# Adapter weights fetched in four chunks beside four tiles, in a routed LoRA kernel

## What is computed

```python
def reference(x, itok, weight):            # x (128, 32, 512), itok (128,), weight (8, 512, 512)
    w = weight[itok]                       # ids are drawn from 3 to 7
    return x + jnp.einsum('bsi,boi->bso', x, w)
```

## Time and profile before

| | |
|---|---|
| median of 3 runs | 105.68 us (105.65 to 105.77) |
| profiled execution | 105.87 us |
| its span, first to last instruction | 104.3 us |
| TensorE busy (matmuls) | 98.8 us, 95% |
| ScalarE busy | 55.9 us, 54% |
| VectorE busy | 52.9 us, 51% |
| GpSimd busy | 42.3 us, 41% |
| moved by DMA | 22.92 MB, mean 220 GB/s |
| mean granted TensorE clock | 0.993 of full |

### The profile page before, as it was taken

How to read it: one execution, slowest core, us unless ns; L and a number is a source line. 1 busy time by engine, 2 the same in 40 slices (tenths; PEclk the granted TensorE clock), 3 DMA queues, 4 the chain that set the end, 5 groups by cost and what they waited for, 6 DMA issues and landing times.

```text
span 104.3 us, 2280 instructions
## 1 busy us (share of the span) xinstructions
PE 98.8 (95%) x437; PEld 79.5 (76%) x437; DVE 52.9 (51%) x107; ACT 55.9 (54%) x103; POOL 42.3 (41%) x58
## 2 busy tenths in 40 slices
PE   5989999999999999999999999999999999999950
PEld 2548888888888888888887888888888888888830
DVE  1569773694076803782248831784477217850000
ACT  5076244594249806592439942695497426952220
POOL 6646305208330761247312774058425530586000
PEclk9999999999999999999999999999999999999997
DMA  1984799939996999789993587648736585354533
GB/s 15 316 229 122 208 233 338 322 86 341 357 316 203 231 356 360 221 140 333 390 314 109 174 259 262 203 126 253 241 106 204 182 262 155 103 188 149 182 101 101
DMA packets 24944, 22.92 MB, mean 220 GB/s; under 512 B 3121, under 2 KB 20018, under 8 KB 24930
## 3 DMA queue, kind: packets, MB, share of 16 engines
q1 hardware_dynamic: 19298, 9.45, 33.2%
q0 software_dynamic: 2608, 8.06, 20.2%
q10 hardware_dynamic: 3024, 5.24, 16.5%
HBM read 17.30 MB, written 8.91 MB: 251 GB/s over the span
## 4 chain that ended last, share of the span: by engine, by line
PE 86%; DMA 3%; ACTq 2%; ACT 2%; SPq 1%; POOL 1%; issue 1%; DVE 1%; POOLq 0%
PE out_ps L527 86%; DMA x_raw<-in_x 3%; ACTq L189 2%; ACT out_tile L344 1%; SPq L179 1%; SPq L185 0%; ACT xt_hi L315 0%; DVE first_from_end L400 0%; POOL ones L253 0%; POOL earlier L257 0%; POOL from_end L250 0%; DVE ids_bf L402 0%; DVE first_at L405 0%; POOL eights L259 0%; POOL key_base L250 0%
## 5 line engine op out<-in xcount | busy, mean ns | idle before, releaser
L287 POOL DMA_INDIRECT out<-out_tile,row_of x31 | 34.9, 1127 | 49.5 <-ACT out_tile L344 45.3
L527 PE MATMUL out_ps<-w_hi,xt_hi 128*128 (+1 forms) x136 | 53.1, 390 | 0.4 <-ACT xt_hi L315 0.4
L527 PE MATMUL out_ps<-w_lo,xt_hi 128*128 (+1 forms) x136 | 52.9, 389 | 0.0
L442 DVE TENSOR_TENSOR xt_lo<-x_raw,xt_hi 128x512 fp32r<-128x512 f32 x34 | 23.7, 696 | 32.2 <-ACT xt_hi L315 31.6
L527 PE MATMUL out_ps<-w_hi,xt_lo 128*128 (+1 forms) x136 | 36.6, 389 | 0.0
L315 ACT ACTIVATE xt_hi<-x_raw 128x512 fp32r<-128x512 f32 (+1 forms) x35 | 21.5, 616 | 26.1 <-DMA x_raw<-in_x 25.9
L527 PEld LDWEIGHTS out_ps<-w_hi,xt_hi 128*128 128x128 f32 x136 | 25.5, 188 | 6.3 <-issue 1.1
L527 PEld LDWEIGHTS out_ps<-w_hi,xt_lo 128*128 128x128 f32 x136 | 25.5, 188 | 5.3
L527 PEld LDWEIGHTS out_ps<-w_lo,xt_hi 128*128 128x128 f32 x136 | 25.5, 188 | 5.3
L337 ACT ACTIVATE w_hi<-w_raw 128x512 fp32r<-128x512 f32 x32 | 18.2, 621 | 12.2 <-DVE w_raw L176 9.1
L344 ACT ACTIVATE out_tile<-out_ps 128x512 f32<-128x512 f32 x34 | 19.9, 585 | 6.1 <-PE out_ps L527 6.1
(11 more groups left out here) (60 smaller groups left out, 10.3 us busy)
## 6 DMA issues: line engine op xcount, KB each, us to landing
x_raw<-in_x SPq DMA_DIRECT2D x130, 64.0 KB, 2.7
w_raw<-in_weight ACTq DMA_DIRECT2D x6, 1024.0 KB
w_raw<-in_weight ACTq DMA_DIRECT2D x6, 256.0 KB, 4.0
w_raw<-in_weight SPq DMA_DIRECT2D x2, 256.0 KB, 3.1
out<-out_tile,row_of POOLq DMA_INDIRECT x31, 3.9
out<-out_tile ACTq DMA_DIRECT2D x6, 64.0 KB, 1.9
out<-out_tile SPq DMA_DIRECT2D x6, 64.0 KB, 2.0
x_raw<-in_x POOLq DMA_DIRECT2D x4, 64.0 KB, 2.7
```

The source lines that it names most:

```text
L287: nc.gpsimd.indirect_dma_start(out=out_rows, out_offset=bass.IndirectOffsetOnAxis(ap=row_of[:, t:t + 1], axis=0), in_=out_tile[n][:, :], i ...
L442: nc.vector.tensor_tensor(xt_lo[t % XT_BUFS][:, :, :, :], x_raw[t % X_BUFS][:, :, :, :].rearrange("p m c r -> p c m r"), xt_hi[t % XT_BUFS ...
L527: return nc.tensor.matmul(out_ps[n][:, :], lefts[left][k][:, c, :, :].rearrange("p m r -> p (m r)"), rights[right][:, bass.ds(rank, 1), c, ...
```

## The change

Ranks 2 to 7 are loaded chunk by chunk, in four steps from `NEEDED_FROM[j] - 6` to `NEEDED_FROM[j] - 3`, each with a wait for the same chunk of the adapter two ranks earlier. The diagonal of these ranks is added two chunks at a time, ahead of chunk 0 and ahead of chunk 2. SyncE issues chunk 3 of rank 0 right behind chunk 1. The semaphores of weight loads are now one for each buffer and chunk.

```diff
-        w0_loaded = [sem(f"w0_loaded{c}") for c in range(CHUNKS)]
-        w1_loaded = [sem(f"w1_loaded{c}") for c in range(CHUNKS)]
-        w_loaded = [sem(f"w_loaded{n}") for n in range(W_BUFS)]
+        w_loaded = [[sem(f"w_loaded{n}_{c}") for c in range(CHUNKS)] for n in range(W_BUFS)]
...
         def wait_w_loaded(eng, rank, c):
-            if rank == 0:
-                eng.wait_ge(w0_loaded[c], 16)
-            elif rank == 1:
-                eng.wait_ge(w1_loaded[c], 16)
-            else:
-                eng.wait_ge(w_loaded[rank % W_BUFS], 16 * (rank // W_BUFS))
+            eng.wait_ge(w_loaded[rank % W_BUFS][c], 16 * (rank // W_BUFS + 1))
...
-            return [j for j in range(2, ADAPTERS) if t == NEEDED_FROM[j] - 5]
+            return [(j, c) for j in range(2, ADAPTERS) for c in range(CHUNKS) if t == NEEDED_FROM[j] - 6 + c]
...
         @block.sync
         def _(sp):
             sp.dma_start(ids_row[:, :], ids.rearrange("(o b) -> o b", o=1)).then_inc(ids_row_loaded, 16)
-            load_rank_0(sp, (1,))
+            load_rank_0(sp, (1, 3))
...
             load_tile(0, first[0:2])
-            load_rank_0(sp, (3,))
             load_tile(1, first[SEQS:2 * SEQS])
...
-            def load_rank(j):
+            def load_chunk(j, c, key):
                 n = j % W_BUFS
-                k = act.value_load(sorted_key[0:1, j:j + 1], min_val=0, max_val=MAX_KEY)
-                act.wait_ge(w_lo_ready, (j - W_BUFS) * CHUNKS + CHUNKS)
-                act.dma_start(w_raw[n][:, :, :], w_t[bass.ds(k & (KEY - 1), 1), :, :, :].rearrange("a c p o -> p (a c) o"),
-                              cond=k >= KEY, max_dma_last_dim=4 * D).then_inc(w_loaded[n], 16)
+                act.wait_ge(w_lo_ready, (j - W_BUFS) * CHUNKS + c + 1)
+                act.dma_start(w_raw[n][:, c, :], w_t[bass.ds(key & (KEY - 1), 1), c, :, :].rearrange("a p o -> (a p) o"),
+                              cond=key >= KEY).then_inc(w_loaded[n][c], 16)
...
-                    act.wait_ge(w_plus_one, c + 1 if j == 1 else CHUNKS + j - 1)
+                    act.wait_ge(w_plus_one, c + 1 if j == 1 else CHUNKS + 2 * (j - 2) + c // 2 + 1)
...
-                for j in weight_loads(t):
-                    load_rank(j)
+                for j, c in weight_loads(t):
+                    if c == 0:
+                        key = act.value_load(sorted_key[0:1, j:j + 1], min_val=0, max_val=MAX_KEY)
+                    load_chunk(j, c, key)
...
-                    elif c == 0:
+                    elif j > 1 and c % 2 == 0:
                         wait_w_loaded(dve, j, c)
-                        add_one(nc.vector, j, slice(0, CHUNKS)).then_inc(w_plus_one, 1)
+                        wait_w_loaded(dve, j, c + 1)
+                        add_one(nc.vector, j, slice(c, c + 2)).then_inc(w_plus_one, 1)
                     split_weight(j, c)
```

More of the change, by code:

```diff
@@ L151, in load_rank_0 @@
             for c in chunks:
-                eng.dma_start(w_raw[0][:, c, :], w_t[FIRST_ADAPTER, c, :, :]).then_inc(w0_loaded[c], 16)
+                eng.dma_start(w_raw[0][:, c, :], w_t[FIRST_ADAPTER, c, :, :]).then_inc(w_loaded[0][c], 16)
         def wait_w_loaded(eng, rank, c):
-            if rank == 0:
-                eng.wait_ge(w0_loaded[c], 16)
-            elif rank == 1:
-                eng.wait_ge(w1_loaded[c], 16)
-            else:
-                eng.wait_ge(w_loaded[rank % W_BUFS], 16 * (rank // W_BUFS))
+            eng.wait_ge(w_loaded[rank % W_BUFS][c], 16 * (rank // W_BUFS + 1))
         def weight_steps(t):
@@ L304, in load_rank_1 @@
                 act.dma_start(w_raw[1][:, c, :], w_t[bass.ds(a, 1), c, :, :].rearrange("a p o -> (a p) o")
-                              ).then_inc(w1_loaded[c], 16)
-            def load_rank(j):
+                              ).then_inc(w_loaded[1][c], 16)
+            def load_chunk(j, c, key):
                 n = j % W_BUFS
-                k = act.value_load(sorted_key[0:1, j:j + 1], min_val=0, max_val=MAX_KEY)
-                act.wait_ge(w_lo_ready, (j - W_BUFS) * CHUNKS + CHUNKS)
-                act.dma_start(w_raw[n][:, :, :], w_t[bass.ds(k & (KEY - 1), 1), :, :, :].rearrange("a c p o -> p (a c) o"),
-                              cond=k >= KEY, max_dma_last_dim=4 * D).then_inc(w_loaded[n], 16)
+                act.wait_ge(w_lo_ready, (j - W_BUFS) * CHUNKS + c + 1)
+                act.dma_start(w_raw[n][:, c, :], w_t[bass.ds(key & (KEY - 1), 1), c, :, :].rearrange("a p o -> (a p) o"),
+                              cond=key >= KEY).then_inc(w_loaded[n][c], 16)
             def x_hi_part(t, chunks):
```

## The result

The change makes the kernel slower by half a per cent: 106.37 us median against 106.03 us, 22 runs of each. The ratio of the executions compared is 1.005 with a 95% interval of 1.0028 to 1.0072, that is 0.30 to 0.76 us. The forecast was no visible change, at 105.65 us. The fastest of the 22 is 105.91 us after and 105.55 us before, 0.36 apart. The profiled execution after took 106.32 us (105.87 before), with a span of 104.6 us (104.3). They are a rough measure: beside the experiments the kernel before ran 17 to 35 times and each variant 6 or 12 times, and the fastest of more executions is lower by luck alone.

A forecast was written before the change was run, and what follows sets the result against it. TensorE's row of product matmuls was taken as the bound. Start 0, gap -0.08, adds and issues 0, tail 0 took the profiled 105.87 us to 105.79; carried to the 105.68 median with half the gain, 105.65, range 105.3 to 106.15.

The forecast's parts named there:

- tail 0 (no edit reaches it): Copy and store of the last tile: no edit touches them, so the change costs 0 there.
- 4.0 us more queue time: ScalarE's queue: nine more live and nine more switched-off chunk issues take 4.0 us, hidden, so cost 0.
- rival 1: Start: chunk 3 ahead of tile 0's x delays the first products, up to 0.67 us; time 106.3, chance 0.16.
- rivals 1 and 2: Start of products: later by up to 0.67 us (106.3, chance 0.16), or earlier by up to 0.47 (105.35, chance 0.21).
- The rule of the ring's order: DMA engines work in order within one ring, so SyncE's half of tile 0's x starts behind chunk 3: 106.3 us.
- the price of 0.67 us: Start: upper end, tile 0's x waits behind the whole chunk 3, 262 KB at 393 GB/s.
- the zero: Landing of tile 0's x at the start: taken as 0, between ends of -0.47 and +0.67 us.
- the split takes the peaks off x's waits: Sign: with loads in four chunks, ScalarE's waits for x lose their peaks above 3 us.
- the 0.08 gap: TensorE's matmuls near 56 us: one tile takes 2.80 instead of 2.72; gain at least 0, at most 0.08, taken as 0.08.
- rival 3: Tiles 11, 15 or 19: ScalarE's order becomes the bound, 0.2 to 0.4 us per live adapter; time 106.3, chance 0.04.
- 0.9 was forecast: VectorE: twelve two-block diagonal adds of 0.42 replace six of 0.684, 0.9 us more busy time.
- the margin: Tile 19: x_hi on ScalarE ends 0.84 us before its first weight load, so 0.82 us of added delay just fits.

The follow-up runs named there:

- experiment 2: Changed kernel with chunk 3 of the first weight back between x of tile 0 and tile 1: ratio 1.010 over only 6 executions.
- experiment 3: Kernel before with 18 idle register loads on ScalarE's queue, no transfer split: ratio 1.010; repeated, 1.0075.
- two idle loads: Changed kernel with two idle register loads on ScalarE's queue, steps 13 and 17: fastest 105.64 us against 105.53 before.
- 6: Kernel before with 20 idle register loads on ScalarE's queue: fastest execution 0.37 us above that of before on its chip.
- 7: Changed kernel with chunk 3 of the first weight in its old place and two idle register loads, run twice: ratios 0.996 and 1.001.
- 8: Version 7 with more warm-up matmuls, 7, 3, 8, 3, 5 in place of 6, 2, 6, 2, 5: ratio 1.004, fastest 105.98 us.
- experiment 1: Kernel before with only chunk 3 of the first weight issued early, right behind chunk 1: ratio 0.998, fastest 105.63 against 105.56 us.
- 4: Changed kernel without the loads of ranks 5 to 7 and the waits for them: ratio 0.997, fastest 105.50 against 105.56 us.
- one: Changed kernel with one idle register load on ScalarE's queue, in step 13: fastest 105.73 us against 105.53 before.
- both long kernels: Kernel before with 18 and with 20 idle register loads: fastest 0.75 and 0.98 us (18, two runs) and 0.37 us (20) above before.

## Why the prediction was wrong

**The step that failed** is one term of the sum: "tail 0 (no edit reaches it)". No edit stands in the tail, but its instructions stand behind those of the edit in ScalarE's program. 54 more recorded instructions moved the last store's register move onto the hole. This costs 0.30 us from copy to landing in the changed kernel's trace (3.58 instead of 3.28). That is shown: the five traces with 54 instructions more have the hole at the 313th instruction (the changed kernel twice, experiment 2, experiment 3 twice), three instructions more put it ahead of the first store instead of the second, and six remove it in all five traces (with two idle loads, 6, both of 7, and 8), on both kernels. The forecast of 4.0 us more queue time was right about the queue (the issues of ranks 2 to 7 take 5.3 us instead of 1.6) and looked only at whether other work hides it, not at where it pushes the code.

Of the 0.72 us between the forecast of 105.65 and the measured 106.37, 0.35 is the base: the three runs of before had a median of 105.68, the 22 have 106.03. And that 106.37 lies beside rival 1's 106.3 is chance, as nothing was late at the first product.

**The other 0 to 0.46 us** of the interval are not settled. In the profiled execution it is 0.32 us of slow first products. They come and go between executions: none slow in the traces of before, experiments 1, 4, 6, one and two idle loads, the second of 7, and 8; 3 to 7 in both traces of the changed kernel, in experiment 2, in the first of 7 and in the second of 3; all 12 of the first tile in the first of 3. The first of 7 and its repeat are the same code and differ, so it is no property of a kernel alone. But all five traces with 54 instructions more have them, and only one of the other nine. Drawn blindly that would come about 3 times in 1,000, and it was noticed afterwards; whether the length of ScalarE's program also bears on the start is untested.

In the repeat of the changed kernel the slow products start 0.43 us apart, nearly twice the usual 0.23. The trace's record of the granted clock has no entry at the start. Its first entry, full clock, begins at 8.36 us in the changed kernel and at 10.20 in the repeat, and the last slow weight load ends at 8.44 and 10.26. In all six traces with slow loads the two times are at most 0.12 us apart; in the eight others the entry begins at 4.87 to 7.59 us, before the first weight load of a product or 0.08 after it. The page's clock row fills the time ahead of the entry with full clock. So the products are slow until full clock is on record, though the warm-up matmuls stand right ahead of them, up to 7.50 us in the changed kernel. That this was TensorE's lower clock of 1.2 GHz is inferred from the distance, as no entry names it. The Trainium skill (TensorE: Matmul & The Clock Gate, section Wait — 56ns, not 53.3ns?) gives 426.7 ns between starts for 512 columns at the lower clock, which agrees with the 0.43.

**Right:** *rivals 1 and 2, the start: neither came true.* In the changed kernel ScalarE began tile 0's x at 7.01 instead of 7.13, although SyncE issued its first x at 4.02 instead of 3.83, and the fastest executions of experiment 1 are 0.07 us apart. The rule of the ring's order, which the prediction names, is not refuted by that. Chunk 3 landed at 5.87 to 6.07 us in the six traces that have it early, and the first of the four landings of tile 0's x came right behind, at 6.02 to 6.41 instead of 5.57 to 5.87. But the last of the four, for which ScalarE waits, came at 6.96 to 7.09, among the 6.77 to 7.46 of the others. The early chunk moved the first landing, as that order would have it, and not the one that counts; so the price of 0.67 us didn't come true and the zero stood.

**Right:** *the split takes the peaks off x's waits* (15.2 us in all against 25.9 before; longest 2.8 instead of 3.4) and closes the 0.08 gap. It was worth more, and once cost 0.5 us, in other executions than in the one that the forecast read: over the five traces with 1 MB loads the middle (start of the third tile to the last copy) of the chain is 0.1, 0.8, 0, 0 and 1.7 us longer than its shortest, over the nine traces with chunks 0 to 0.02 in seven, 0.1 in one and 0.5 in one. "At most the 0.08" was too small a bound for a kernel, as it was read from one execution. That the chunks are what spares x these stalls is suggested by the counts, not shown: single traces, and the times tell no gain.

**Right in kind, too small a chance:** *rival 3*, ScalarE's order at tile 15. Its two waits are 1.09 us each, to the hundredth, and the half add takes 0.42. VectorE is busy for 1.0 us more, where 0.9 was forecast.

```profile
ACT xt_hi L306 <- DMA x_raw<-in_x: 15.2, 13, 2.8
ACT w_hi L328 <- DVE w_raw L169: 11.9, 11, 1.1
```

```profile
L169 DVE TENSOR_TENSOR w_raw<-w_raw,identity 128x256 f32<-128x256 f32 x12 | 5.0, 418 | 0.0
```

These two views are the waits and the groups by form of the changed kernel; the second answers to the earlier trace rows, with 12 x 0.418 = 5.0 us. In the changed kernel's own two traces the margin held; of the nine with chunks one lost 0.5 us at tile 15 and that of experiment 8 lost 0.1.

## What to carry to other kernels

In a kernel bound from start to end by one engine, read what the edit does to the length of every engine's program, and look at what stands unhidden at its end: a term of 0 for "untouched" code needs the same proof as any other. When a change that should be neutral costs 0.2 to 0.4 us, subtract the traces piece by piece (first product, middle, last copy to last landing) before looking for a cause in the edit. A margin read from one execution is one draw; a starved transfer may be 0.1 us late in it and 1.7 us in the next.

## What the runs showed of the hardware

An engine's queue stops without a wait at fixed places in its program. Counted over the recorded instructions of the two queues, the first as 0, with the idle time ahead of each:

```
before, SyncE:    79th 0.42 us   207th 0.35 us   335th 0.34 us   425th 0.44 us
after, SyncE:     79th 0.42 us   207th 0.35 us   335th 0.34 us   425th 0.44 us
after, ScalarE:   313th 0.32 us  (also in both long kernels and in experiment 2)
with two idle loads, ScalarE: 191st 0.33 us, 313th 0.33 us, none between the last stores
```

SyncE has these four in all fourteen traces; other pauses, which differ from trace to trace, are not listed. The first three are 128 instructions apart. The fourth comes 90 behind the third and ScalarE's 313th 122 behind its 191st, both with branches between, which may jump over code that is then not recorded. With two idle loads the 313th instruction is the wait for the last product. Mostly an engine has work queued or waits anyway, so the hole shows only at a place like the last store.

The page lists a queue for instructions in both kernels, and in this one 9 packets and 0.07 MB on q14 and 6 packets and 0.10 MB on q8, 8 and 16 KB each. In all eleven traces with the hole at ScalarE's 313th instruction a packet of 8 KB on q14 starts 0.65 to 1.00 us after the hole's end, at 102.90 in the changed kernel; in the three without it (before, experiments 1 and 4) the last such packet starts behind the span. So the hole and a fetch of code come together. That the hole is the switch from one block to the next is argued from the distances and these times, not shown. The Trainium skill (Advanced Engine Details and Errata, section ISA Cache) speaks of instruction cache lines of 16 KB or 256 instructions; the distance in this trace is 128. By these figures of the Trainium skill an instruction takes 64 bytes and a packet of 8 KB holds 128 of them, an estimate, which agrees with the distance.
